# Two graph-attention networks on one core: the loops over edge batches written out on every engine, and the gather lists read from the SBUF table itself

## The chip, the cores and the metric

One NeuronCore of a Trainium2 chip runs the whole kernel. The metric is the device time of one execution in microseconds (us); lower is better.

## What is computed

The reference takes 3125 nodes with 256 features and 53125 edges, sorted by target node. It runs one graph network of two attention layers (4 heads, then 1 head), adds the input and normalises each row, then a second network of one attention layer with 8 heads and edge features, adds and normalises again. In each layer

```python
e = leaky_relu(alpha_s[src] + alpha_d[dst], 0.2)      # + edge term in the third layer
m = segment_max(e, dst)
w = exp(e - m[dst])
out = segment_sum(h[src] * (w / segment_sum(w, dst)[dst]), dst) + bias
```

where `h = x @ W`, per head. So there are three attention layers, which the kernel numbers 0, 1 and 2.

## The kernel before

**Tiling.** The 3125 nodes are 25 blocks of 128 rows, one node per partition. The edges are cut into 440 slots of 128 edges, so that all targets of a slot lie in one block. Eleven slots (B) form a batch, and a layer has 40 batches (K). For every slot GpSimd gathers the 128 source rows from a table in DRAM with one indirect DMA (L1128), TensorE sums the weighted rows into their targets by a product with a one-hot matrix (L1485), and VectorE adds the result to the block's sums in SBUF (L766). In layers 0 and 1 the scores need only a small transposed computation for each batch. In layer 2 every slot also has an edge encoding: four matmuls (L1496, L1499), a ReLU on ScalarE (L1280), a product and a reduction on VectorE (L772, L778).

**Order of the work.** Each engine has its own instruction stream, with the order of a batch's period written out by hand (the table `AT` says at which slot a step is put). VectorE's period begins with `rescale` (L747), reads the block numbers of the next batch's slots into registers once (`load`, L787), and uses them as offsets into `sums`. Four batches are in flight: a period works on batch t and on its successors t+1, t+2 and t+3. Buffers such as `rows` are rings of three (RING), and the batch's place in the ring is `u`.

**The loops.** On VectorE, ScalarE, TensorE and GpSimd `batches` runs the period. Batches 0 to 35 of a layer are 12 turns of a hardware loop, whose body holds three periods, one for each `u`. Batches 36 to 39 follow the loop, written out, with batch numbers known when the program is built. In the loop a semaphore's target value depends on the loop's register, so waits compare against registers, which instructions ahead of them compute (L295, L304), and the loop ends in a compare and a branch (L340). Batch 36 is the only written-out one that still does all of a full period's steps, since it still has three batches behind it. SyncE loads what a batch needs (`meta`), also in a loop over batches 3 to 38.

**The gather lists.** The row numbers of all 440 slots lie in SBUF in `index_all`. The gathers of batches 0 to 2 read them from there. From batch 3 on, SyncE first copies the batch's 11 columns to `index`, a ring of three, and GpSimd waits for that copy (`s_index`) and reads its list from the ring. A batch's gathers also wait until TensorE has used the rows of the batch three before it in the same buffer (`agg`).

Of the kernel before, what the change touches and what calls it, by code (L numbers as in the profile page):

```python
# [21 lines left out]
I32 = mybir.dt.int32  # L22
# [5 lines left out]
P = 128  # L28
# [8 lines left out]
B = 11  # L37
K = SLOTS // B
# [3 lines left out]
RING = 3  # L42
# [55 lines left out]
def gat_kernel(nc, x, src, dst, edge_attr, w1, as1, ad1, b1, w2, as2, ad2, b2, w3, as3, ad3, edge_w, edge_b, b3, out):  # L98
    ctx = ExitStack()
    with ctx:  # L100
        def sb(name, shape, dt=F32):
            return ctx.enter_context(nc.sbuf_tensor(name, shape, dt))
# [4 lines left out]
        def sem(name):  # L107
            return ctx.enter_context(nc.semaphore(name))
# [21 lines left out]
        flags = sb("flags", [8 * B, RING, 5, P])  # L130
        chain = sb("chain", [1, RING, 2, 8, B + 1])
        carry = sb("carry", [2, RING, P])
        index = sb("index", [P, RING, B], I32)
        index_all = sb("index_all", [P, SLOTS], I32)
        blk = sb("blk", [1, K * BPAD], I32)
        ntab = sb("ntab", [P, BLOCKS, 16])
# [144 lines left out]
        s_dpad = sem("s_dpad")  # L281
        s_w0 = sem("s_w0")
        s_parts = sem("s_parts")
        s_index = [[sem(f"s_index{l}_{u}") for u in range(RING)] for l in range(3)]
        s_meta = [[sem(f"s_meta{l}_{u}") for u in range(RING)] for l in range(3)]
        s_rows = [[sem(f"s_rows{l}_{u}") for u in range(RING)] for l in range(3)]
        s_tab = [[sem(f"s_tab{l}_{u}") for u in range(TROW)] for l in range(3)]
# [9 lines left out]
        def need_apart(eng, *waits):  # L297


            for w, c in waits:  # L300
                if isinstance(w, str):
                    need(eng, w, c)
                else:
                    eng.wait_ge(w, c)  # L304
                if not isinstance(c, int):
                    eng.sem_inc(s_passed[eng], 1)
# [29 lines left out]

        def batches(eng, body):

            loops = (K - 3) // RING
            with eng.Fori(0, loops) as j:  # L340
                for u in range(RING):
                    body(Batch(j, u), K)
            for k in range(loops * RING, K):
                body(Batch(k // RING, k % RING), K - k)

        def block_regs(eng, tag):
# [545 lines left out]
        def _(sp):  # L892
# [42 lines left out]
            for l in range(3):  # L935
                H = HEADS[l]

                def meta(t, l=l, H=H):
                    if not isinstance(t.j, int) or t.k >= RING:

                        need_apart(sp, ("fac", l * K + t.k - 2), ("hot", l * K + t.k - 2),
                                   ("mask" if SELF[l] else "diff", l * K + t.k - 2),
                                   (s_rows[l][t.u], t.j * (16 * B)))
                    if not isinstance(t.j, int) or t.k >= RING:
                        sp.dma_start(index[:, t.u, :], index_all[:, bass.ds(t.k * B, B)]).then_inc(s_index[l][t.u], 16)
                    for h in range(H):
                        sp.dma_start(flags[h * B:(h + 1) * B, t.u, :, :].rearrange("p t e -> p (t e)"),
                                     flags_d[bass.ds(t.k * B, B), :]).then_inc(s_meta[l][t.u], 16)
                    for i, at in ((0, 1), (1, 0)):
                        row = chain_d[i:i + 1, bass.ds(t.k * B, B)]  # L950
                        sp.dma_start(chain[0:1, t.u, i, 0:H, at:at + B],
                                     row.unsqueeze(1).to_broadcast([1, H, B])).then_inc(s_meta[l][t.u], 16)
                    sp.dma_start(carry[:, t.u, :], carry_d[bass.ds(t.k * B, 1), :, :].rearrange("a r e -> (a r) e")).then_inc(s_meta[l][t.u], 16)
                    sp.dma_start(locb[:, t.u, :], loc_d[bass.ds(t.k * B * P, B * P)].partition_broadcast(P)
                                 ).then_inc(s_meta[l][t.u], 16)
                    if l == 2:
                        for i in range(3):
                            sp.dma_start(attrT[9 * i:9 * i + 9, t.u, :],
                                         attrT_d[:, bass.ds(t.k * B * P, B * P)]).then_inc(s_meta[l][t.u], 16)
# [18 lines left out]
                else:  # L978
                    need(sp, "add", l * K * B)
                    first_metas()  # L980
                    for b in range(BLOCKS):
                        write(b, b % TROW)
                with sp.Fori(1, K // RING) as j:
                    for u in range(RING):
                        meta(Batch(j, u))
                for k in range(K // RING * RING, K):
                    meta(Batch(k // RING, k % RING))
                if l < 2:

# [16 lines left out]
        def _(pool):  # L1006
# [62 lines left out]
            for l in range(3):  # L1069
# [49 lines left out]

                def gather(t, l=l):  # L1120
                    old = not isinstance(t.j, int) or t.k >= RING
                    if old:
                        need_apart(pool, (s_index[l][t.u], t.j * 16))
                    for lo, hi in GATHERS:
                        if old:
                            need_apart(pool, ("agg", (t.k + (l * K - 3)) * B + hi))
                        for s in range(lo, hi):
                            g.indirect_dma_start(out=rows[:, t.u, s, 0:ROW[l]], out_offset=None, in_=table[l],  # L1128
                                                 in_offset=bass.IndirectOffsetOnAxis(ap=index[:, t.u, s:s + 1] if old else index_all[:, t.k * B + s:t.k * B + s + 1], axis=0)
                                                 ).then_inc(s_rows[l][t.u], 16)  # L1130
                for k in range(RING):
                    gather(Batch(0, k))
# [443 lines left out]
```

## Time and profile before

| what | us |
|---|---|
| median of 3 runs | 2442.32 (2439.75 to 2443.36) |
| the profiled execution, its own time | 2431.28 |
| its span, first to last instruction | 2429.4 |
| layer 0, from its first `rescale` to its last gather | 131 to 670 |
| layer 1, from its first gather to its last | 774 to 1333 |
| layer 2, from its first `rescale` to that of batch 36 | 1494 to 2332 |

The positions are in us from the start of the span. The rows further down come from this one execution; PE is TensorE, DVE VectorE, ACT ScalarE, POOL GpSimd and SP SyncE; DVEq is VectorE's instruction queue, where register operations show. "issue" as the releaser of an engine means that the engine waited for no other engine or transfer that the trace shows. Between the layers lie stages that are written out already and that the change leaves alone.

### The profile page before, as it was taken

The numbers are of one execution on the slowest core, as the hardware profiler recorded it, in microseconds if no ns is written. First come the engines' busy times: TensorE is split into PE (matmuls) and PEld (weight loads), VectorE is DVE, ScalarE is ACT, GpSimd is POOL, SyncE is SP. The second block draws the span as 40 slices with busy tenths as digits, with TensorE's granted clock in tenths as the row PEclk, the third lists the DMA queues.
The fourth block names the chain that finished last, engine by engine and source line by source line (L and its number), as shares of the span: only waits on it lengthen the run. The fifth ranks groups of instructions, "written<-read, shape, count | busy, mean of one in ns | idle before, by whom it ended". The sixth has DMA issues, their size and how long they took to land.

```text
span 2429.4 us, 49749 instructions
## 1 busy us (share of the span) xinstructions
PE 1753.2 (72%) x8878; PEld 1055.8 (43%) x8879; DVE 1844.4 (76%) x5643; ACT 1018.6 (42%) x3430; POOL 1535.4 (63%) x1675
## 2 busy tenths in 40 slices
PE   4368777778765677777787667778777777787783
PEld 3245444444433354444454433444444444444441
DVE  5478888888896566666666766888888888888888
ACT  2233444344424354454454443444444444444444
POOL 2567777777745777777777474565555555655553
PEclk9578888888868788888887776788787787888876
DMA  5644444444612444544446122333333333333321
GB/s 153 150 129 133 139 139 143 137 136 138 192 35 72 131 131 131 137 131 132 136 131 175 57 71 79 86 107 92 91 103 86 104 89 94 107 88 97 102 69 54
DMA packets 145430, 273.39 MB, mean 113 GB/s; under 512 B 55607, under 2 KB 80306, under 8 KB 145289
## 3 DMA queue, kind: packets, MB, share of 16 engines
q0 software_dynamic: 64704, 182.91, 27.6%
q1 hardware_dynamic: 77452, 86.16, 11.8%
q10 hardware_dynamic: 3158, 3.20, 0.4%
q14 instruction: 96, 0.79, 0.1%
q8 instruction: 20, 0.33, 0.1%
HBM read 255.35 MB, written 17.20 MB: 112 GB/s over the span
## 4 chain that ended last, share of the span: by engine, by line
PE 30%; DVE 27%; issue 19%; POOL 9%; DVEq 6%; ACT 4%; DMA 4%; SPq 2%; POOLq 0%; ACTq 0%
PE bank L1485 15%; POOL rows L1128 7%; DVE sums L766 5%; PE bank L1499 5%; PE bank L1419 3%; DVE prod L772 3%; DVE dots L778 3%; DVE rows L755 3%; DVEq L787 3%; PE bank L1496 2%; DMA rows<-table,index 2%; DVEq L766 1%; ACT rows L1273 1%; DVE adsum L639 1%; DVE onehotT L629 1%
## 5 line engine op out<-in xcount | busy, mean ns | idle before, releaser
L1128 POOL DMA_INDIRECT rows<-table,index x1221 | 1190.4, 975 | 636.6 <-PE bank L1485 321.6
L1485 PE MATMUL bank<-rows,onehot 128*128 128x264 f32 (+1 forms) x2640 | 1015.6, 492 | 198.2 <-DVE sums L766 143.6
L766 DVE TENSOR_TENSOR sums<-sums,bank 128x264 f32 (+1 forms) x1320 | 552.6, 419 | 190.8 <-PE bank L1485 139.2
L1485 PEld LDWEIGHTS bank<-rows,onehot 128*128 128x128 f32 x2640 | 510.1, 230 | 380.3 <-DVE sums L766 207.2
L1273 ACT ACTIVATE rows<-rows,wgt 128x33 f32<-128x33 f32 (+2 forms) x1520 | 443.9, 369 | 0.2
L1280 ACT ACTIVATE prod<-bank 128x256 f32<-128x256 f32 x440 | 168.3, 383 | 408.3 <-PE bank L1499 406.9
L1228 ACT CAST onehot<-bank 128x768 f32<-128x768 bf16 x240 | 178.0, 743 | 331.5 <-PE bank L1419 328.6
L1499 PE MATMUL bank<-late,onehotT 128*128 x1320 | 259.8, 314 | 0.0
L755 DVE TENSOR_TENSOR rows<-rows,wgt 128x260 f32<-128x260 f32 (+2 forms) x560 | 240.1, 429 | 3.6 <-ACT wgt L1266 3.6
L772 DVE TENSOR_TENSOR prod<-prod,bank 128x256 f32<-128x256 f32 x440 | 182.5, 415 | 46.6 <-ACT prod L1280 43.7
L1419 PE MATMUL bank<-identb,onehotT 128*128 128x128 bf16 x1320 | 160.0, 278 | 37.3 <-DVE onehotT L629 30.5
L778 DVE TENSOR_REDUCE dots<-prod 128x8 f32<-128x256 f32 x440 | 181.6, 413 | 2.4
L1496 PE MATMUL bank<-edgew,late 30*128 30x256 bf16 x440 | 136.9, 311 | 60.9 <-DVE onehotT L629 60.1
L1419 PEld LDWEIGHTS bank<-identb,onehotT 128*128 128x128 bf16 x1320 | 125.1, 128 | 76.9 <-issue 52.2
L1441 PE MATMUL bank<-ident,score 128*44 128x128 f32 (+2 forms) x200 | 46.6, 302 | 151.1 <-DVE score L656 150.5
L1499 PEld LDWEIGHTS bank<-late,onehotT 128*128 128x128 bf16 x1320 | 101.7, 104 | 78.8 <-issue 30.6
L1128 POOL DMA_INDIRECT rows<-table,index_all x99 | 98.2, 992 | 59.2 <-issue 29.1
L1235 ACT COPY scoreT<-bank 44x256 f32<-44x256 f32 (+2 forms) x120 | 39.6, 330 | 227.1 <-PE bank L1441 220.4
L1496 PEld LDWEIGHTS bank<-edgew,late 30*128 30x128 bf16 x440 | 44.1, 100 | 187.3 <-DVE onehotT L629 85.7
L1140 POOL TENSOR_TENSOR rows<-rows,wgt 128x264 f32<-128x264 f32 x160 | 102.6, 672 | 33.2 <-ACT wgt L1266 32.5
L1258 ACT ACTIVATE expT<-expT 44x256 f32<-44x256 f32 (+2 forms) x120 | 45.4, 378 | 171.3 <-DVE expT L727 171.1
L1402 PE MATMUL bank<-wts,rows 128*128 128x264 f32 (+2 forms) x300 | 97.1, 456 | 18.6 <-DVE wts L388 11.0
(196 smaller groups left out, 1937.7 us busy)
## 6 DMA issues: line engine op xcount, KB each, us to landing
locb<-loc_d SPq DMA_DIRECT2D x120, 352.0 KB
rows<-table,index POOLq DMA_INDIRECT x1221
flags<-flags_d SPq DMA_DIRECT2D x520, 27.5 KB
table<-rows SPq DMA_DIRECT2D x25, 136.0 KB, 1.7
table<-rows SPq DMA_DIRECT2D x25, 134.0 KB, 2.4
late<-table SPq DMA_DIRECT2D x1, 3300.0 KB, 18.0
table<-rows SPq DMA_DIRECT2D x25, 129.5 KB, 2.0
late<-table SPq DMA_DIRECT2D x1, 3212.5 KB, 18.3
```

The source lines that it names most:

```text
L755: done(v.tensor_tensor(r, r, w.to_broadcast([P, H, n]), ALU.mult), "mulv")
L766: done(v.tensor_tensor(a, a, ps_sum[l][s % len(ps_sum[l])][:, 0:VV], ALU.add), "add")
L772: done(v.tensor_tensor(prod[:, s % 3, :], prod[:, s % 3, :], ps_enc[s % 3][:, D:2 * D], ALU.mult), "prod")
L778: done(v.tensor_reduce(dots[:, t.u, s, :], prod[:, s % 3, :].rearrange("p (h c) -> p h c", h=8), AX.X, ALU.add), "dot")
L1128: g.indirect_dma_start(out=rows[:, t.u, s, 0:ROW[l]], out_offset=None, in_=table[l], in_offset=bass.IndirectOffsetOnAxis(ap=index[:, t.u, ...
L1228: done(a.copy(onehot[:, t.u, lo:hi, :].rearrange("p s e -> p (s e)"), ps_hotb[l][g][:, 0:(hi - lo) * P]), "hotT")
L1273: i = a.activation(r, r, ACT.Copy, scale=wgt[:, t.u, h * B + s:h * B + s + 1])
L1280: done(a.activation(prod[:, s % 3, :], ps_enc[s % 3][:, 0:D], ACT.Relu), "enc")
L1419: r = m.transpose(ps_hotb[l][g][:, (s - lo) * P:(s - lo + 1) * P], onehotT[:, t.u, s * P:(s + 1) * P], identb[:, :])
L1485: done(m.matmul(ps_sum[l][s % nb][:, 0:VV], onehot[:, t.u, s, :], rows[:, t.u, s, 0:VV], start=True, stop=True), "agg")
L1496: m.matmul(p[:, 0:D], attrT[:, t.u, s * P:(s + 1) * P], edgew3[:, :], start=True, stop=True)
L1499: r = m.matmul(p[:, D:2 * D], onehotT[:, t.u, s * P:(s + 1) * P], hnode3[:, bass.ds(b, 1), i, :].rearrange("p a f -> p (a f)"), start=(i = ...
```

## The change

`batches` no longer makes a loop: all 40 batches of a layer are written out on the four compute engines, and SyncE's loop over `meta` likewise. Every batch number is then a constant, and so is every wait's target. The copies to `index`, the ring and its semaphores go, and all gathers read `index_all`. The reading of block numbers into registers (L787) stays.

```diff
-        index = sb("index", [P, RING, B], I32)
...
-        s_index = [[sem(f"s_index{l}_{u}") for u in range(RING)] for l in range(3)]
...
         def batches(eng, body):
 
-            loops = (K - 3) // RING
-            with eng.Fori(0, loops) as j:
-                for u in range(RING):
-                    body(Batch(j, u), K)
-            for k in range(loops * RING, K):
+            for k in range(K):
                 body(Batch(k // RING, k % RING), K - k)
...
-                    if not isinstance(t.j, int) or t.k >= RING:
-                        sp.dma_start(index[:, t.u, :], index_all[:, bass.ds(t.k * B, B)]).then_inc(s_index[l][t.u], 16)
...
-                with sp.Fori(1, K // RING) as j:
-                    for u in range(RING):
-                        meta(Batch(j, u))
-                for k in range(K // RING * RING, K):
+                for k in range(RING, K):
                     meta(Batch(k // RING, k % RING))
...
                     old = not isinstance(t.j, int) or t.k >= RING
-                    if old:
-                        need_apart(pool, (s_index[l][t.u], t.j * 16))
                     for lo, hi in GATHERS:
                         if old:
                             need_apart(pool, ("agg", (t.k + (l * K - 3)) * B + hi))
                         for s in range(lo, hi):
-                                                 in_offset=bass.IndirectOffsetOnAxis(ap=index[:, t.u, s:s + 1] if old else index_all[:, t.k * B + s:t.k * B + s + 1], axis=0)
+                                                 in_offset=bass.IndirectOffsetOnAxis(ap=index_all[:, t.k * B + s:t.k * B + s + 1], axis=0)
```

## Rows read from the trace of the kernel before

**Rows 1.** The page, part 1: each engine's busy time.

```profile
PE 1753.2 (72%) x8878; PEld 1055.8 (43%) x8879; DVE 1844.4 (76%) x5643; ACT 1018.6 (42%) x3430; POOL 1535.4 (63%) x1675
```

**Rows 2.** Busy time by stage, all engines; the stretch's length follows its bounds.

```profile
core 0: us, PE busy (x) PEld busy (x) DVE busy (x) ACT busy (x) POOL busy (x), PEclk, DMA share, GB/s
131.00:670.00 539.00, 417.11 (x2085) 259.38 (x2085) 447.22 (x1454) 219.18 (x778) 400.14 (x407) 0.84 0.50 142
774.00:1333.00 559.00, 417.41 (x2150) 262.57 (x2151) 353.46 (x1224) 259.61 (x721) 424.82 (x440) 0.81 0.50 136
...
1494.00:2332.00 838.00, 647.17 (x3530) 366.04 (x3530) 690.48 (x2017) 359.49 (x1260) 473.03 (x535) 0.80 0.34 95
```

**Rows 3.** POOL's groups from 774 to 1333: count, busy, mean ns, idle before.

```profile
L1128 POOL DMA_INDIRECT rows<-table,index x407 | 393.3, 966 | 124.1 <-issue 114.0 <-PE bank L1485 10.1
L1128 POOL DMA_INDIRECT rows<-table,index_all x33 | 31.5, 955 | 25.4 <-DMA table<-rows 15.6 <-issue 9.5 <-PE bank L1485 0.3
```

**Rows 4.** POOL in order of time, layer 1: start, duration, in brackets idle before.

```profile
773.98 0.98 POOL L1128 DMA_INDIRECT rows<-table,index_all  x1 [15.65 <-DMA table<-rows]
...
814.30 0.95 POOL L1128 DMA_INDIRECT rows<-table,index_all  x1 [0.30 <-issue]
815.55 0.95 POOL L1128 DMA_INDIRECT rows<-table,index  x1 [0.30 <-issue]
...
1331.71 0.95 POOL L1128 DMA_INDIRECT rows<-table,index  x1 [0.30 <-issue]
```

**Rows 5.** POOL's waits, 146 to 670: total us, times, longest.

```profile
POOL rows L1128 <- PE bank L1485: 23.4, 43, 2.2
```

**Rows 6.** DVE's waits in layer 2, 1520 to 2330.

```profile
DVE sums L766 <- PE bank L1485: 40.1, 40, 1.3
DVE sums L747 <- issue: 33.7, 11, 3.3
```

**Rows 7.** The chain around one turn of layer 2's loop: start, us, what.

```profile
1773.62 0.07 DVEq L340
1773.68 2.91 issue
```

**Rows 8.** The instruction queues' packets in layer 2's loop, 1520 to 2330.

```profile
q14 instruction: 57, 0.47, 0.2%
q8 instruction: 3, 0.05, 0.0%
```

**Rows 9.** DVE in order of time: `rescale` of batches 0, 33, 36 and 37, layer 2.

```profile
1494.78 0.43 DVE L747 TENSOR_TENSOR sums<-sums,bank 128x264 f32 x1 [1.50 <-issue]
...
2264.86 0.43 DVE L747 TENSOR_TENSOR sums<-sums,bank 128x264 f32 x1 [3.02 <-issue]
...
2331.82 0.43 DVE L747 TENSOR_TENSOR sums<-sums,bank 128x264 f32 x1
...
2353.24 0.42 DVE L747 TENSOR_TENSOR sums<-sums,bank 128x264 f32 x1
```

**Rows 10.** DVE's waits in layer 0, 146 to 650.

```profile
DVE sums L766 <- PE bank L1485: 24.2, 32, 1.1
...
DVE sums L747 <- issue: 2.9, 6, 0.5
```

**Rows 11.** Busy time by batch in layer 2: batches 31, 33 and 36.

```profile
2218.34:2240.18 21.84, 16.70 (x98) 9.49 (x98) 19.74 (x57) 10.06 (x35) 13.21 (x16) 0.96 0.35 101
...
2264.86:2287.16 22.30, 17.67 (x98) 10.22 (x98) 19.09 (x57) 9.95 (x35) 10.47 (x13) 0.81 0.30 82
...
2331.82:2353.24 21.42, 17.15 (x99) 10.43 (x99) 18.94 (x56) 9.95 (x35) 14.00 (x16) 0.82 0.28 77
```

**Rows 12.** DMA issues by line: the copies of the gather lists.

```profile
index<-index_all SPq DMA_DIRECT2D x111, 5.5 KB
```

**Rows 13.** The instruction queue's packets from 1360 to 1500, which is written out.

```profile
q14 instruction: 7, 0.06, 0.2%
```

**Rows 14.** DVE's waits from 1360 to 1500.

```profile
DVE sums L747 <- issue: 1.5, 1, 1.5
```

## The prediction, made before the changed kernel ran

> **What bounds the kernel now.** I read the page's busy shares first, only to see that they don't decide: VectorE leads with 76%, TensorE has 72%, GpSimd 63% [rows 1]. Busy time by stage does. In layer 1 VectorE is busy for 353 of 559 us, but GpSimd issues all 440 gathers of the layer in that stretch [rows 2]. A gather takes 0.966 us and the idle time ahead of it is 0.30 us, 124.1 us over 407 [rows 3]. The few waits named after TensorE come to about the same 0.30 us each, so they are the pitch and no wait. From 773.98 to 1331.71 GpSimd never stops [rows 4]: 439 steps in 557.7 us, 1.27 us each. Layer 1 is bound by the issue of gathers.
>
> Layer 0 is nearly so. From 146 to 670 GpSimd waits 43 times for TensorE's sums, 23.4 us in all [rows 5]. 43 × 0.30 = 12.9 us of that is pitch; 10.5 us are real waiting for rows to be used.
>
> Layer 2 is another case: 838 us for 36 batches, GpSimd busy 473 us, VectorE 690 us [rows 2]. There VectorE's stream sets the pace. Its waits show the largest single thing that is no work: 33.7 us ahead of `rescale`, in 11 places of about 3.06 us, with nothing to wait for [rows 6]. The chain tells where they come from: VectorE's queue executes the loop's last instruction, L340, and then stands still for 2.91 us [rows 7]. It is the turn of the loop, and 12 turns have 11 jumps back. Instruction packets arrive all through this stretch, 57 on the queue q14 [rows 8]. I take the gap for the fetch of the loop's first instructions after each jump.
>
> **The change, part by part, layer 2.** Its three parts here:
>
> *The jumps.* 11 × 3.06 = 33.7 us go from VectorE's stream. Does something else end the wait later? At the loop's exit, where the branch isn't taken, `rescale` of batch 36 at 2331.82 has no idle time ahead of it, while that of batch 33 has 3.02 us [rows 9]. So nothing waits behind the gap. I take all 33.7 us.
>
> *The price of a jump, weighed against a rule.* The row shows 2.91 us for one turn of layer 2 [rows 7]. The Trainium skill, page "Advanced Engine Details and Errata", section "Control Flow Timing", puts a compare-and-branch at about 108 ns; by that alone the 11 jumps would cost 1.2 us, and the forecast would be 32 us later. Its page "Runtime: NRT & Kernel Launch", section "Instruction fetch mechanics", adds that a taken branch to a target outside the window of fetched pages stalls for a fetch, which fits the row. In layer 0 the whole wait "issue" ahead of `rescale` is 2.9 us in 6 places [rows 10]: there a turn costs next to nothing, and I expect no such gain from layers 0 and 1.
>
> *Constants for registers.* Waits against constants need fewer queue instructions, on all engines at once, and they can go with the instruction they guard. The trace has one sample: batch 36 is written out and does a full period. It takes 2353.24 − 2331.82 = 21.42 us [rows 9]. A batch in the loop, without gaps: batches 0 to 35 take 2331.82 − 1494.78 = 837.0 us; less 33.7 for the jumps and 3 for the slow start of batch 0 (an estimate) it is 800 us, 22.2 us each. Batches 33 to 35 agree: 2331.82 − 2264.86 = 66.96, 22.3 us each. Work is the same, VectorE busy 19.09 us in batch 33 and 18.94 in batch 36 [rows 11]. So 0.8 us × 36 = 28.8 us. One sample is weak. The bounds: 0.2 us (7 us in all), since batch 31 too ran in 21.84 us with a granted clock of 0.96 [rows 11], and 1.4 us (50 us), which is under half of the 3.2 us that VectorE isn't busy in a batch of 22.3. I take the sample.
>
> *What hides less then.* TensorE is busy 17.2 to 17.7 us in such a batch, at a granted clock of 0.81 or 0.82 (a mean over its two levels, 1.2 and 2.4 GHz), and ScalarE 9.95 [rows 11]. Both fit under 21.4 us. GpSimd's 14.0 us do too.
>
> **Layers 0 and 1.** The turn of GpSimd's loop and its register work are hidden by the gathers: the idle time ahead of a gather stays 0.30 us everywhere in layer 1 [rows 3, 4]. The list's address changes nothing: the gather at 814.30 reads `index_all`, the next one `index`, both take 0.95 us after 0.30 us [rows 4], and the means are 955 and 966 ns [rows 3]. Layer 1: 0, bounds ±3 us for the few gathers that are longer than 0.95 us (440 × 0.95 = 418 against 424.8 busy).
>
> In layer 0 a quicker period on VectorE and TensorE brings forward the sums that GpSimd waits for, at most the 10.5 us worked out above; VectorE itself loses 24.2 us to TensorE there, both of them little slower than the gathers [rows 10]. With 0.8 us less in a batch I expect most of it back, 8 us; bounds 0 and 10.5.
>
> **SyncE and the copies.** 111 copies of 5.5 KB are no longer issued [rows 12], and GpSimd's wait for them goes. It never showed: every wait of the gathers is the pitch or TensorE [rows 3, 5]. The cover is that a list is copied while the ring's earlier batches are gathered. The metas behind each copy on SyncE's queue start a little earlier, for nobody. 0 us.
>
> **The sum.** 33.7 + 28.8 + 8 + 0 + 0 = 70.5 us. The profiled execution took 2431.3 us, of which 2429.4 are span, so it would take 2361. It ran 11 us below the median of the runs. Against the median 2442.3 the forecast is 2442.3 − 70.5 = 2372 us.
>
> **Rivals.**
>
> *The straight stream can't be fetched fast enough (slower).* Now every instruction has to be brought in once, in all three layers, and each late packet would stand an engine still for the 2.9 us of [rows 7]. In layer 2's loop 60 packets came in about 35 batches [rows 8], 1.7 for a batch. Were each of 1.7 × 40 = 68 exposed, it would be 197 us, less 70.5: 2569 us. From 24 exposed ones on (70.5 / 2.9) the change loses. For it: many more instructions are fetched. Against it: between 1360 and 1500 all is written out, 7 packets came on q14 [rows 13], and the longest wait of VectorE without another engine or a transfer behind it is 1.5 us [rows 14]; and in the loop itself all but the jump's own packets came unnoticed, 60 packets to 11 gaps [rows 6, 8]. The same Runtime page says that crossing a block's boundary is mostly hidden; by that this rival falls. Chance 0.04.
>
> *Only the jumps pay.* Batch 36 was quick for being late: SyncE has nothing more to load then. The constants would bring some 0.1 us a batch, layer 0 nothing: 2442.3 − 37 = 2405 us. For it: one sample, a DMA share of 0.28 against 0.30 to 0.35 [rows 11]. Against: it has fewer queue instructions for the same work. Chance 0.14.
>
> *The gap isn't the jump.* By the branch price of the errata page, something at the batch boundary would stand there in any case, such as the four waits of `rescale`; then only 28.8 + 8 us come, 2405.5 us. Against it: two in three boundaries of the loop have no gap, and neither has its exit [rows 6, 9]. Chance 0.02.
>
> *TensorE takes the gap back.* It catches up during the 3 us, and without them the period stays bound by it: VectorE waits 40.1 us for its sums in this layer already [rows 6]. If they grow by the 33.7 us and the constants bring nothing, it is 2442 us, no change. Against: 17.7 us of TensorE work for 22.3 us. Chance 0.03.
>
> *More than forecast.* The constants help by 1.4 us a batch and layer 0 in full: 33.7 + 50 + 10.5 = 94 us, 2348 us. Chance 0.09.
>
> The forecast has the rest, 0.68, for 2355 to 2395.
>
> **The range.** Its low end is the sum of the high bounds with 3 us from layer 1: 33.7 + 50 + 10.5 + 3 = 97, 2345 us. Its high end is 33.7 + 7 + 0 − 3 = 38, 2404 us; I move it to 2408, so that the two cases at 2405 lie inside. It leaves out the first and the fourth rival and the outer part of "more", about 0.1 in all. A measurement of this kernel tells 0.2% (5 us) from nothing. Slower takes the first rival, 0.04; within 0.2% the fourth, 0.03; faster the rest, 0.93.
>
> **What the profile after will show.** In layer 2 no idle time of 3 us ahead of `rescale`; its `rescale` instructions 21.4 us apart; in layer 1 the gathers still 1.27 us apart, from first to last about 558 us; in layer 0 GpSimd's waits for TensorE shorter by 8 us; more packets on the instruction queues, without engines idle for them. The prediction is wrong if gaps of 3 us turn up at places without a wait, if batches of layer 2 stay at 22.2 us, or if layer 1 gets shorter.

## The result, and the profile after

The changed kernel takes 2353.27 us (median of 4 runs, 2352.5 to 2355.57), the kernel before 2441.03 us on the same chip (4 runs, 2437.94 to 2443.36). The ratio is 0.9643 with a 95% interval of 0.9626 to 0.9659: 87.8 us less. The forecast was 70.5 us less, 2372 us, with a range of 2345 to 2408.

The profiled execution has a span of 2351.5 us, 77.9 less than that of before. So some 10 us of the 87.8 show in no trace: the profiled execution of before took 2431.28 us, 9.8 under the 2441.03 here (11 under the median that the prediction had), and the one of after took 2353.31 us, which is its median.

The page of the changed kernel, span and part 1, against [rows 1]:

```profile
span 2351.5 us, 42182 instructions
PE 1702.8 (72%) x8878; PEld 1045.5 (44%) x8878; DVE 1847.3 (79%) x5642; ACT 1018.0 (43%) x3430; POOL 1539.9 (65%) x1675
```

VectorE's work did not get less: it is busy for 1847.3 us, before for 1844.4; only its idle time went. TensorE does the same 8878 matmuls in 1702.8 busy us where it took 1753.2; its granted clock, a mean over the two levels of 1.2 and 2.4 GHz, is 0.807 over the execution against 0.796, and 0.85 in layer 2 against 0.80. That comes back below. The busy time by stage, which answers to [rows 2]; the stretches here follow each other and cover layer 0, layer 1, the step between, layer 2 and the tail:

```profile
core 0: us, PE busy (x) PEld busy (x) DVE busy (x) ACT busy (x) POOL busy (x), PEclk, DMA share, GB/s
135.00:664.00 529.00, 413.20 (x2097) 257.96 (x2096) 445.76 (x1452) 219.84 (x781) 400.77 (x408) 0.83 0.51 146
664.00:1319.00 655.00, 468.01 (x2362) 301.15 (x2362) 442.68 (x1429) 295.98 (x878) 464.91 (x491) 0.79 0.43 124
...
1480.00:2255.00 775.00, 613.27 (x3530) 358.84 (x3529) 693.71 (x2017) 358.45 (x1260) 484.55 (x535) 0.85 0.36 104
2255.00:2351.50 96.50, 49.89 (x203) 28.05 (x203) 81.28 (x261) 40.60 (x127) 39.32 (x53) 0.68 0.17 53
```

Measured from the same instruction to the same instruction in both traces (lines of after are 6 to 13 lower):

```
stretch                                              before    after   difference
layer 0, gather at 135.74 to the last (669.58)        533.8    524.2      -9.7
layer 1, first gather to last                         557.7    555.1      -2.7
layer 2, rescale of batch 0 to rescale of batch 36    837.0    774.3     -62.7
```

What ended VectorE's waits in and around layer 2, 1440 to 2270, against [rows 6] (total us, times, longest):

```profile
DVE sums L760 <- PE bank L1472: 31.8, 38, 1.1
DVE prod L766 <- ACT prod L1267: 18.9, 69, 1.2
DVE ends L683 <- PE bank L1435: 12.7, 37, 0.5
...
DVE sums L741 <- issue: 1.5, 2, 1.2
```

The 33.7 us ahead of `rescale` (now L741) are gone (1.2 of the 1.5 us left is the wait ahead of batch 0), and the wait for TensorE's sums is 31.8 us where it was 40.1. GpSimd's waits in layer 0, 146 to 660, against [rows 5]:

```profile
POOL rows L1115 <- issue: 111.2, 365, 0.3
POOL rows L1115 <- PE bank L1472: 14.6, 34, 1.4
```

34 × 0.30 us of the second row are the pitch between gathers, so 4.4 us are waiting; before it was 10.5. Layer 1 is still a row of gathers. GpSimd's group there, 760 to 1322, against [rows 3] (count, busy, mean ns, idle before):

```profile
L1115 POOL DMA_INDIRECT rows<-table,index_all x440 | 422.2, 960 | 149.7 <-issue 123.4 <-DMA table<-rows 16.0 <-PE bank L1472 10.4
```

The instruction queues' packets in layer 2, 1430 to 2260, against [rows 8]:

```profile
q8 instruction: 39, 0.64, 0.3%
q14 instruction: 54, 0.44, 0.2%
```

93 packets where 60 were, and no engine shows an idle time near 3 us for one: from batch 1 of layer 2 on the longest that ends with no other engine or transfer is 0.6 us on VectorE, 0.7 on ScalarE and 0.5 ahead of a matmul. So far every row does what the prediction said. One place does not. VectorE and then GpSimd at the head of batch 22 of layer 2, in order of time:

```profile
1950.97 0.42 DVE L741 TENSOR_TENSOR sums<-sums,bank 128x264 f32 x1
1951.49 0.59 DVE L623 TENSOR_SCALAR onehotT<-locb,pidx 128x1408 bf16<-128x1408 bf16 x1
1951.99 2.99 DVE L671 TENSOR_TENSOR_SCAN top<-flags,top 88x128 f32<-88x128 f32 x1
1954.91 0.40 DVE L760 TENSOR_TENSOR sums<-sums,bank 128x264 f32 x1
```

```profile
1951.33 0.94 POOL L1115 DMA_INDIRECT rows<-table,index_all  x1 [0.30 <-issue]
1952.28 2.41 POOL L1127 TENSOR_TENSOR rows<-rows,wgt 128x264 f32<-128x264 f32 x4
```

The backward scan of the edges' tops (L671, L677 before), 0.41 us where nothing is beside it, took 2.99 us and ended 0.3 us after GpSimd's four multiplications did (1954.98 and 1954.69). It is the only one of the 36 that took so long. In 33 batches it took 0.85 us, as in this one:

```profile
1738.75 0.85 DVE L671 TENSOR_TENSOR_SCAN top<-flags,top 88x128 f32<-88x128 f32 x1
```

```profile
1739.23 2.83 POOL L1127 TENSOR_TENSOR rows<-rows,wgt 128x264 f32<-128x264 f32 x4
```

That collision turned out to decide the experiments on the jumps.

### The profile page after: what moved, and what is told of

Its sections match the earlier page's. It is cut to its first block, busy times and chain, and to the rows that moved or that the text cites. A ratio compares the mean times of both kernels' runs of the same rounds, so it can differ in the third digit from the quotient of the medians.

```text
span 2351.5 us, 42182 instructions
## 1 busy us (share of the span) xinstructions
PE 1702.8 (72%) x8878; PEld 1045.5 (44%) x8878; DVE 1847.3 (79%) x5642; ACT 1018.0 (43%) x3430; POOL 1539.9 (65%) x1675
## 4 chain that ended last, share of the span: by engine, by line
DVE 31%; PE 28%; issue 16%; POOL 13%; DVEq 4%; DMA 3%; SPq 2%; ACT 2%; ACTq 0%; POOLq 0%
PE bank L1472 15%; POOL rows L1115 12%; DVE sums L760 8%; PE bank L1486 4%; DVE prod L766 4%; DVE rows L749 3%; PE bank L1406 3%; DVE dots L772 3%; DMA rows<-table,index_all 2%; PE bank L1483 2%; DVEq L781 2%; DVEq L760 1%; DVE onehotT L623 1%; PE bank L1419 1%; DVE adsum L633 1%
## 5 line engine op out<-in xcount | busy, mean ns | idle before, releaser
L1115 POOL DMA_INDIRECT rows<-table,index_all x1320 | 1283.2, 972 | 615.0 <-issue 346.5
L1472 PE MATMUL bank<-rows,onehot 128*128 128x264 f32 (+1 forms) x2640 | 989.6, 483 | 211.9 <-DVE sums L760 174.3
L1472 PEld LDWEIGHTS bank<-rows,onehot 128*128 128x128 f32 x2640 | 510.3, 229 | 371.0 <-issue 246.4
L1486 PE MATMUL bank<-late,onehotT 128*128 x1320 | 253.2, 308 | 0.0
L749 DVE TENSOR_TENSOR rows<-rows,wgt 128x260 f32<-128x260 f32 (+2 forms) x560 | 241.2, 431 | 3.5 <-ACT wgt L1253 3.5
L766 DVE TENSOR_TENSOR prod<-prod,bank 128x256 f32<-128x256 f32 x440 | 182.1, 414 | 27.8 <-ACT prod L1267 27.4
L772 DVE TENSOR_REDUCE dots<-prod 128x8 f32<-128x256 f32 x440 | 181.5, 413 | 2.4
L1428 PE MATMUL bank<-ident,score 128*44 128x128 f32 (+2 forms) x200 | 51.6, 330 | 124.9 <-DVE score L650 124.9
L1127 POOL TENSOR_TENSOR rows<-rows,wgt 128x264 f32<-128x264 f32 x160 | 112.8, 729 | 32.3 <-ACT wgt L1253 31.6
L1428 PEld LDWEIGHTS bank<-ident,score 128*44 128x44 f32 (+2 forms) x200 | 17.1, 110 | 174.6 <-DVE score L650 171.7
```

The source lines that it names most:

```text
L749: done(v.tensor_tensor(r, r, w.to_broadcast([P, H, n]), ALU.mult), "mulv")
L766: done(v.tensor_tensor(prod[:, s % 3, :], prod[:, s % 3, :], ps_enc[s % 3][:, D:2 * D], ALU.mult), "prod")
L772: done(v.tensor_reduce(dots[:, t.u, s, :], prod[:, s % 3, :].rearrange("p (h c) -> p h c", h=8), AX.X, ALU.add), "dot")
L1472: done(m.matmul(ps_sum[l][s % nb][:, 0:VV], onehot[:, t.u, s, :], rows[:, t.u, s, 0:VV], start=True, stop=True), "agg")
L1486: r = m.matmul(p[:, D:2 * D], onehotT[:, t.u, s * P:(s + 1) * P], hnode3[:, bass.ds(b, 1), i, :].rearrange("p a f -> p (a f)"), start=(i = ...
```

## The experiments

Each ratio is against the kernel before on the same chip in the same set of runs. Three chips' sets had the kernel before at 2439 to 2441 us. Two others had it at 2837 and 2838 us, with every kernel some 16% longer at a granted clock of 0.69 to 0.72 against 0.78 to 0.81; what makes these chips slower stays open. Layer spans are compared only within one kind. On the slower chips there is no profile of the kernel before, so the kernel with the hint, whose time is some 0.2% from it, stands in for it there.

### The jumps: a hint, and a longer body

**e1_hint, e1b_hint, e7_hint_again.** The kernel before, and VectorE's three loops get a hint that has the loop's head fetched before the jump. It adds one instruction to each loop, and nothing else:

```
-            with eng.Fori(0, loops) as j:
+            with nc.Fori(0, loops, 1, engines=[eng.engine],
+                         hint_back_edge=eng is nc.vector or eng.engine == nc.vector.engine) as j:
```

> The kernel before with one instruction added at the head of each of VectorE's three loops: a hint that its branch back will be taken, so that the target's instructions are fetched ahead. Loops, register waits and gather lists stay. If the 2.9 us after each jump of layer 2 are the fetch of the loop's head (my theory), the 11 gaps ahead of rescale go and the kernel is 30 to 35 us faster than before, 0.986 of its time; VectorE's waits named issue ahead of rescale in layer 2 fall from 33.7 us to under 3. If the gap is something else that stands at the batch boundary, the gaps stay and the time is that of before. If TensorE takes the gap back, the gaps go and the time is still that of before. Layers 0 and 1 don't move.

> The kernel with the fetch hint on VectorE's loops again, in the hope of a chip that grants TensorE the clock that the first two profiles had (0.80); on the chip of the first run it was 0.69, the kernel before took 2838 us, and the gaps went without any gain. At a clock of 0.80 my theory expects 25 to 35 us less than before (0.986 to 0.990), since there VectorE's stream sets layer 2's pace. If TensorE takes the gap back at any clock, the time is that of before.

> The fetch hint on VectorE's loops once more, for a chip that grants the clock of the first measurement (before at about 2441 us). There my theory expects 25 to 35 us less than before, 0.986 to 0.990. Where the kernel before takes 2837 us again, the time of before, as in the two runs already made.

Ratios: 1.0013 (0.9997 to 1.0029) and 1.0021 (1.0002 to 1.004) on the chips at 2838 and 2837 us, and 1.0093 (1.0059 to 1.0128) on a chip at 2441, where it is 2462.88 us. The first was expected to be 30 to 35 us faster and was not; the last, expected 25 to 35 us faster, is 22 us slower. The gaps went all the same. VectorE's waits in layer 2 of e7_hint_again, 1510 to 2290:

```profile
DVE prod L772 <- ACT prod L1280: 44.4, 88, 1.2
DVE sums L766 <- PE bank L1485: 36.6, 39, 1.3
DVE sums L747 <- issue: 5.5, 11, 0.5
```

11 waits of 0.5 us where 11 of 3.06 stood, so 28.2 of the 33.7 us are gone, and with them the packets: 2 on q14 from 1530 to 2350, where [rows 8] has 57. Yet layer 2 is 856.2 us long against 837.0. The gap is fetch time, and to take it away made the kernel slower.

**e2_body6.** The kernel before, six batches to a turn in place of three on the four compute engines: the 11 jumps of each layer fall to 5.

```
-            with eng.Fori(0, loops) as j:
-                for u in range(RING):
-                    body(Batch(j, u), K)
+            with eng.Fori(0, loops // 2) as j:
+                for u in range(2 * RING):
+                    body(Batch(j * 2, u), K)
```

> The kernel before with six batches to a turn of the loop in place of three, on the four compute engines: 6 turns and 5 jumps in a layer, still with register waits. If the gap is a fetch that comes with a loop body too long to stay in the engine's instruction memory, layer 2 has 5 gaps of 2.9 us in place of 11 (18 us less), and now VectorE also stands still for about 2.9 us after each of 5 jumps in layers 0 and 1, where a turn was free. Layer 1 is bound by the gathers and hides it, layer 0 hides most: 10 to 20 us faster than before, 0.992 to 0.996. If the gap has nothing to do with the body's length, layers 0 and 1 show no gap, and layer 2 has 5.

Ratio 1.0007 (0.9987 to 1.0027), where 0.992 to 0.996 was expected. Layer 2 was 886.6 us against 909.1 with the hint, but now VectorE stands still at each of the 5 jumps in all three layers. From the branch to the next instruction of VectorE's queue it is 2.84 to 3.56 us in layer 0, 3.40 to 3.89 in layer 1, 3.50 to 4.21 in layer 2. In the kernel before, the same distance is 0.22 to 0.30 us in layers 0 and 1, and 2.73 to 3.02 in layer 2. ScalarE's queue does likewise in layer 2: 2.47 to 2.85 us, where it is 0.18 in the kernel before. VectorE's waits in layer 1, 1000 to 1600, of e2_body6, and the packets of the same stretch:

```profile
DVE sums L747 <- issue: 20.8, 16, 4.2
```

```profile
q14 instruction: 35, 0.29, 0.2%
```

The same packets with the hint and the short body, in the same stretch:

```profile
q14 instruction: 1, 0.01, 0.0%
```

The layer does not matter, the length of the body does. Counted in the traces, a turn of VectorE's loop before has 278 instructions in layer 0, 257 in layer 1 and 369 in layer 2, its queue's own among them; with six batches it has 552, 510 and 734. The two shortest jump in 0.3 us, all others in 2.7 us or more. ScalarE's turn in layer 2 has 195 before and 387 with six batches. So a short body stays and a long one is fetched anew in every turn; between 278 and 369 no run has a body.

### Which engines, and the copies

**e4_vector_only, f4_vector_only_again.** VectorE's three loops alone are written out. **e5_all_but_vector.** Those of TensorE, ScalarE and GpSimd alone (with `!=`).

```
+            if eng.engine == nc.vector.engine:
+                for k in range(K):
+                    body(Batch(k // RING, k % RING), K - k)
+                return
             loops = (K - 3) // RING
```

> The kernel before with VectorE alone written out; TensorE, ScalarE, GpSimd and SyncE keep their loops and register waits. If VectorE's own stream set the pace of layer 2, nearly all of the gain comes: 33.7 us for the jumps, most of 28.8 us for the constants and some of layer 0, 55 to 75 us faster than before, 0.970 to 0.977. If the constants pay through the other engines (TensorE's register operations above all), only the jumps' 34 us come, 0.986.

> The reverse of VectorE alone: TensorE, ScalarE, GpSimd and SyncE... of these the first three are written out, VectorE (and SyncE) keep the loop, its jumps and register waits. At a clock of 0.80 the gaps ahead of rescale stay and VectorE keeps setting the pace of layer 2: 0 to 12 us faster than before. If the constants pay on TensorE, it is 20 us faster or more; on a chip with the clock at 0.69, where TensorE sets the pace, I expect that: 30 us or more.

> VectorE's three loops alone are written out, all other engines keep theirs; run before on a chip where every kernel took 16% longer. It differs from the kernel with the branch hint in VectorE's constants alone (waits and batch numbers known in the program), and from the changed kernel in the other engines' constants. If the constants on VectorE carry the gain, layer 2 stands near 775 to 800 us; if those of the other engines carry it, near 856 us, as with the hint; half and half, about 815 us. Layer 0 should be at the kernel before's 534 us if its gain is GpSimd's, TensorE's and ScalarE's.

**e3_ring_kept.** All loops written out, but the lists are still copied by SyncE to the ring `index`, and GpSimd waits for them.

> Everything written out as in the changed kernel, but the gather lists are still copied to the ring of three and GpSimd waits for the copies: the change without its second part. By my theory the copies were hidden and cost nothing: the time of the changed kernel, 0.964 of before, within 0.2%. If the copies or their wait mattered, it is slower than the changed kernel, up to the 20 us that layers 0 and 1 and the rest gained beyond layer 2.

**e6_changed_again.** The changed kernel once more.

> The changed kernel itself, beside the others. In the runs so far the kernel before took 2837 us, with a granted clock near 0.69, where the first measurement had 2441 us and 0.80. If the chip is again such a one, I expect the ratio of the written-out kernel with the ring kept, 0.967, within 0.003, since the copies of the lists cost nothing; at the clock of the first measurement 0.964.

```
kernel                 ratio (95% interval)        chip's before   layer 0   layer 1   layer 2
e3_ring_kept           0.9672 (0.9626 to 0.9717)   2838            634.7     711.5     840.5
e4_vector_only         0.9840 (0.9817 to 0.9863)   2838            662.9     701.7     862.1
e1_hint                1.0013 (0.9997 to 1.0029)   2838            666.3     702.7     909.1
e5_all_but_vector      0.9891 (0.9857 to 0.9925)   2837            640.2     692.7     902.3
e1b_hint               1.0021 (1.0002 to 1.0040)   2837            670.9     702.6     906.9
e6_changed_again       0.9665 (0.9629 to 0.9701)   2441            523.6     556.2     776.1
f4_vector_only_again   0.9758 (0.9738 to 0.9777)   2439            532.0     556.2     793.8
the kernel before      1                           2441            533.8     557.7     837.0
```

Expected were 0.970 to 0.977 for VectorE alone, which came on the faster chip (0.9758) and not on the slower one (0.9840); 30 us or more on a slow chip for the other three, which came (31 us by the ratio); and the change's own ratio for the last two, which came within their intervals. Layer 0's gain is not VectorE's: with VectorE alone written out it is 532.0 us, with all of them 523.6; on the slower chips the other three engines alone bring it from about 668, with the hint, to 640. Layer 2's is VectorE's first: 43 of 63 us. The kernel that keeps ring and copies gains as much as the change, within the intervals (on another chip, and with an interval of 13 us to either side, so that less than that can't be told). Its layer 1 is the longest of its kind at 711.5 us, but behind its first gather every wait there ends on the semaphore of TensorE's sums, and none on that of a copy.

### The collision

In all kernels so far GpSimd's four weight multiplications of layer 2 stand at the head of a batch, behind the last gathers of the batch before. Three kernels, the one before, the one with the hint and the changed one, each with one edit: the next batch's multiplications are issued ahead of the last group of three gathers, in the middle of VectorE's batch.

```
                 def gather(t, l=l, first=None):
                     ...
                     for lo, hi in GATHERS:
+                        if first is not None and lo == GATHERS[-1][0]:
+                            muls(first)
...
-                    for s in OWN[l]["P"]:
-                        mul(t, s)
-                    if left > 3:
-                        gather(t.after(3))
+                    if left > 3:
+                        gather(t.after(3), first=t.after(1))
+                    elif left > 1:
+                        muls(t.after(1))
+                muls(Batch(0, 0))
```

> The kernel before, loops kept, with one edit: GpSimd's four weight multiplications of the next batch in layer 2 stand ahead of the last group of three gathers of a batch, in place of at the head of the next batch. There VectorE's backward scan of the last edges can run beside them: it took 538 ns on average in the kernel before, 1279 ns with the branch hint, against 410 ns when it runs alone. Theory A (the scan loses its time to GpSimd's multiplications): the scan falls to about 0.42 us and layer 2 gains up to 36 x 0.12 = 4 us where nothing else waits; the three gaps per turn of the loop stay. Theory B (the mean of the scan has another cause, its input arrives late): the scan stays at 538 ns and the time does not change. The last three gathers of a batch leave some 2.4 us later; if that is what the scores wait for, the kernel gets up to 36 x 2.4 = 86 us slower.

> The kernel with the branch hint on VectorE's loops and the same move of GpSimd's multiplications. With the hint alone layer 2 was 856.2 us against 837 and the scan took 44.8 us in place of 18.8. Theory A (the collision eats the gap's time): the scan falls to 0.42 us, 30 us come back, and layer 2 ends at about 826 us or under, some 10 us or more below the kernel before, as the 33.7 us of gaps are now gained in part. Theory B (what the gap hid is TensorE's and ScalarE's lateness, and the long scan only stands where VectorE would have waited anyway): the scan gets short and layer 2 stays within 5 us of 856, with the waits for the banks and for ScalarE's products grown by as much.

> The changed kernel with the same move of GpSimd's multiplications. Its scan took 897 ns on average, 31.4 us in 35 batches. Theory A: the scan falls to about 0.42 us, layer 2 gains up to 17 us and the kernel is at about 2340 us, the fastest of all. Theory B: the scan gets short, the wait for the banks that TensorE fills grows by as much, and the time stays at 2355 us within 5 us.

Medians 2443.78, 2430.8 and 2374.63 us; ratios 1.0021 (1.0005 to 1.0037), 0.9967 (0.9952 to 0.9983), 0.9724 (0.9702 to 0.9746). Only the second did what one of its theories said: its layer 2 is 819.7 us, under the 826 of theory A. The first was to gain up to 4 us and lost 5; the third was to end at 2340 or 2355 us. VectorE's scan L677 in layer 2, 1510 to 2290, in the kernel before, with the hint, and with hint and move (count, busy, mean ns, idle before):

```profile
L677 DVE TENSOR_TENSOR_SCAN top<-flags,top 88x128 f32<-88x128 f32 x34 | 18.4, 540 | 0.0
```

```profile
L677 DVE TENSOR_TENSOR_SCAN top<-flags,top 88x128 f32<-88x128 f32 x32 | 40.7, 1273 | 0.0
```

```profile
L677 DVE TENSOR_TENSOR_SCAN top<-flags,top 88x128 f32<-88x128 f32 x34 | 13.9, 408 | 0.0
```

And how it comes about, first VectorE and then GpSimd, at one turn of the loop with the hint:

```profile
1716.66 0.43 DVE L747 TENSOR_TENSOR sums<-sums,bank 128x264 f32 x1 [0.50 <-issue]
1717.13 0.59 DVE L629 TENSOR_SCALAR onehotT<-locb,pidx 128x1408 bf16<-128x1408 bf16 x1
1717.63 3.07 DVE L677 TENSOR_TENSOR_SCAN top<-flags,top 88x128 f32<-88x128 f32 x1
```

```profile
1717.05 0.95 POOL L1128 DMA_INDIRECT rows<-table,index  x1 [0.30 <-issue]
1718.02 2.41 POOL L1140 TENSOR_TENSOR rows<-rows,wgt 128x264 f32<-128x264 f32 x4
```

The same place in the kernel before:

```profile
1704.09 0.42 DVE L778 TENSOR_REDUCE dots<-prod 128x8 f32<-128x256 f32 x1
1707.60 0.43 DVE L747 TENSOR_TENSOR sums<-sums,bank 128x264 f32 x1 [3.09 <-issue]
1708.06 0.59 DVE L629 TENSOR_SCALAR onehotT<-locb,pidx 128x1408 bf16<-128x1408 bf16 x1
1708.57 0.85 DVE L677 TENSOR_TENSOR_SCAN top<-flags,top 88x128 f32<-88x128 f32 x1
```

```profile
1706.36 2.79 POOL L1140 TENSOR_TENSOR rows<-rows,wgt 128x264 f32<-128x264 f32 x4
```

In the kernel before GpSimd had begun its multiplications in the gap and was 2.2 us into 2.8 us of them when the scan began (1708.57 − 1706.36). The scan met only their end, here and in 8 more batches behind a jump. Without the gap it meets them all. Both times it ends 0.27 us after they do (1720.70 and 1720.43, 1709.42 and 1709.15).

How much it costs hangs on a tenth of a microsecond. With the hint 11 scans began 0.36 to 0.39 us ahead of GpSimd's first multiplication and took 3.06 to 3.08 us. In the changed kernel 31 began 0.47 to 0.50 us ahead and took 0.85 (1738.75 and 1739.23 above); there GpSimd's first multiplication got longer instead, 0.86 us where it has some 0.65. The one that began 0.29 us ahead is that of batch 22, with its 2.99 us.

The two tables below are means over batches 0 to 35 of layer 2, worked out from the starts of VectorE's instructions, in us. The first gives a batch's length by its place in the turn of three, with the scan's own mean in brackets (written-out kernels have no turn):

```
                        1st              2nd              3rd (ends with the jump)
the kernel before       22.60 (0.74)     22.33 (0.40)     24.82 (0.46)
hint                    26.16 (2.85)     22.44 (0.42)     22.75 (0.50)
before, moved           22.66 (0.41)     22.43 (0.41)     25.08 (0.41)
hint, moved             22.91 (0.41)     22.51 (0.40)     22.88 (0.41)
```

The hint takes 2.07 us from the batch that ends with the jump and gives 3.56 to the one that follows. With the multiplications out of the way it takes 2.20 and gives 0.25.

The second cuts a batch into five pieces of VectorE's stream: from `rescale` over the scan to the first product (L772) behind it; on to the product behind the batch's fourth weight multiplication (L755), with waits for ScalarE's products in it; from there to the sum (L766) that waits for TensorE's bank; the rest; and the last step, from the batch's last reduction (L778) to the next `rescale`, with the jump in it:

```
                        head    to middle   wait    rest    last step   batch
the kernel before       2.81    11.07       1.59    6.43    1.34        23.25
hint                    3.35    11.63       1.57    6.68    0.56        23.78
before, moved           2.84    10.98       1.57    6.64    1.36        23.39
hint, moved             2.84    11.07       1.55    6.75    0.56        22.77
VectorE alone           2.79    11.14       1.47    6.30    0.35        22.05
changed                 2.77    10.84       1.27    6.28    0.35        21.51
changed, moved          2.71    10.84       1.32    6.73    0.34        21.94
```

The hint wins 0.78 in the last step, loses 0.54 in the head, where the scan is, 0.56 behind it and 0.25 in the rest. Behind the head TensorE, which works in order, had stood for the scan's result, which it never did in the kernel before; that is 0.29 us a batch. TensorE's wait in layer 2 with the hint, 1510 to 2290:

```profile
PE bank L1448 <- DVE top L677: 10.6, 10, 1.1
```

With the move, the first two losses are gone (2.84 and 11.07); the last stays (6.75), as the move costs something there itself (6.64 against 6.43 without the hint). Of the 19 us by which the hint lengthened layer 2, the first batch of a turn has 12 × 3.56 = 42.7, from which the saved gaps go. The granted clock in layer 2 was 0.77 with the hint, against 0.80 before and 0.80 with hint and move; what it added by itself stays open.

In the changed kernel the move gains nothing. The head falls by 0.06 only, though its scan falls from 883 to 413 ns, since what comes next there waits for ScalarE's product anyway: 0.16 us behind a scan of 0.85, 0.73 behind one of 0.41. And in the rest of the batch, where GpSimd's multiplications now are, 0.45 is lost. VectorE's fifth weight multiplication and its forward scan (L663) meet them there and take 755 and 520 ns on average, where they took 423 and 414. At one place, VectorE and then GpSimd:

```profile
1703.32 0.74 DVE L749 TENSOR_TENSOR rows<-rows,wgt 128x264 f32<-128x264 f32 x1
1703.98 0.41 DVE L766 TENSOR_TENSOR prod<-prod,bank 128x256 f32<-128x256 f32 x1
1704.31 0.52 DVE L663 TENSOR_TENSOR_SCAN top<-flags,scoreT 88x128 f32<-88x128 f32 x1
```

```profile
1702.51 2.74 POOL L1129 TENSOR_TENSOR rows<-rows,wgt 128x264 f32<-128x264 f32 x4
```

So theory A holds for the hint. For the change neither does: the scan's time was hidden, as B says, but the move brought new collisions that neither theory had. f3_after_moved is 16 us slower than e6_changed_again (on another chip; the ratios are 0.9724 and 0.9665), and the changed kernel stays the fastest of all.

## Why the prediction was right

**The jumps: 33.7 us, and it was 35.6.** The last step of a batch fell from 1.34 to 0.35 us, 36 × 0.99 = 35.6 us in layer 2, in the changed kernel and in the one with VectorE alone alike, and in neither did another piece grow by more than 0.07. The 11 gaps are 33.7 of it; the rest lies in last steps that had no gap. That the gap is the fetch after a jump is shown from both sides: by the hint (gap and packets go) and by the longer body (gap and packets come, in layers that had none). A jump took 0.22 to 0.30 us where the body was short, and 2.7 to 4.2 where it was long. The Trainium skill, page "Runtime: NRT & Kernel Launch", section "Instruction fetch mechanics", has the stall after a jump out of the fetched window, and these runs agree. The Trainium skill's page "Advanced Engine Details and Errata", section "Control Flow Timing", has about 108 ns for a compare-and-branch; by that alone the 11 jumps would have given 1.2 us, and they gave 33.7.

But the argument "nothing waits behind the gap" was too quick. It rested on the loop's exit, where the gap was missing and nothing came in its place. 28.2 of the same 33.7 us, taken away by the hint alone, left the kernel 22 us slower. What stood behind it was no wait, and so the views of waits of the kernel before could not show it: an instruction of VectorE that gets longer when it runs beside one of GpSimd's. The prediction had no rival for it; its only case on the slower side, at 0.04, was another mechanism. That the change did not fall into it is luck as far as the prediction goes, for its reasoning would have taken the hint's 28 us for a gain just as well. In the changed kernel most scans start 0.1 us earlier against GpSimd than behind the hint's jumps. They take 0.85 us, which a wait for ScalarE's product covers, and only one takes 2.99; in that batch the head is 4.60 us long where most have 2.64. Had they all been so, it would have been some 70 us (35 × 1.96, an estimate from these two numbers), most of the gain.

**The constants: 28.8 us, and it was 27.** What is left of the batch fell by (23.25 − 1.34) − (21.51 − 0.35) = 0.75 us, × 36 = 27 us. The one sample, batch 36, was a good one: its 21.42 us against a mean of 21.51 after. The experiments split it. VectorE written out brings (23.25 − 1.34) − (22.05 − 0.35) = 0.21 us a batch, 7.6 us; the rest of the change 22.05 − 21.51 = 0.54, 19.4 us, of which 0.20 in the wait for TensorE's bank and 0.30 on the way to it. The prediction had not said whose constants, and expected at e4_vector_only most of the 28.8 us from VectorE's.

That these 19.4 us are all the constants' is not shown, for the granted clock in layer 2 rose with them: 0.80 before, 0.82 with VectorE alone, 0.85 with the change. Within the changed kernel, of batches 1 to 35 without batch 22, the 11 with the highest granted clock (0.91 on average) take 20.84 us and the 11 with the lowest (0.82) 21.79. That is about 0.1 us for each 0.01, so 0.03 would be 0.3 of the 0.54 us (an estimate from these rows). Whether shorter waits raised the clock, which would make that part the constants' after all, no run tells.

**Layer 0: 8 us, and it was 9.7.** GpSimd's waiting fell by 10.5 − 4.4 = 6.1 us; the rest lies in the gathers' own length, 396.2 us in sum where they took 399.7, which the prediction did not have. Its reason was half right: sums come earlier, but not from VectorE's side (532.0 us with VectorE alone against 524).

**Layer 1: 0 ± 3, and it was 2.7.** 439 steps of 1.264 us in place of 1.270: gathers of 960 ns in place of 966 and 955. It is inside the bounds, though the prediction's last sentence took a shorter layer 1 for a sign of being wrong.

**The copies: 0.** e3_ring_kept has them all and its ratio is 0.9672 (0.9626 to 0.9717) against 0.9643 and 0.9665. They cost nothing that these runs can tell, which is to within some 13 us.

**The sum.** 62.5 us in layer 2 were forecast, 62.7 came, 1.9 more from the last steps and 1.8 less from the rest; with 8 and 0 against 9.7 and 2.7, and 2.8 us at the edges of the layers, the profiles differ by 77.9. The time's further 10 us are the distance between a profiled execution and its median. It had been seen (11 us below) and carried over whole, to 2372 from the 2361 that the sum gave for the profiled execution; after the change the distance is nothing. Of the 19 us by which the forecast was high, that is 11. Why the profiled execution of before was so quick is open.

**The rivals.** *The stream can't be fetched* is refuted: 93 packets and no gap. *Only the jumps pay* is refuted: outside the last step a batch fell by 0.75 us and not by 0.1. With the hint it was the jumps that did not pay. *The gap isn't the jump* is refuted by e2_body6 and the hints. *TensorE takes the gap back*: with the multiplications moved, the hint should gain 0.80 us a batch in the last step and gains 0.62 in the whole (22.77 against 23.39); 0.18 is taken back, a quarter. The 13 us between 2443.78 and 2430.8 are what the jumps alone are worth then, in the profiles' layer 2 it is 22.4 us, but the profiled execution with the hint ran 8 us below its median. With the hint alone more than all was taken back, most of it through the long scan.

## What to carry to other kernels

To remove an idle gap is not yet to win it: look also at what another engine does meanwhile, and which instruction of yours will then run beside it; a view of waits does not show it, a row whose mean duration grows does. A loop body that was too long to stay fetched cost 2.7 to 4.2 us a turn here, and a hint or straight code removed it; whether that pays is read from the batch that follows. Cutting a batch into pieces by the starts of one engine's instructions, over all batches, splits a gain between its pieces better than sums of waits; the granted clock belongs beside every such piece.

## What the runs showed of the hardware that was not expected

- VectorE's scan over 88x128 elements (L677) takes 0.41 us alone. Beside GpSimd's multiplications of 128x264 it takes 0.85 us when it began 0.44 to 0.50 us ahead of them, and 2.96 to 3.09 when it began 0.27 to 0.40 us ahead, over all traces here; then it ends 0.3 us after the last of the four.
- VectorE's own multiplication L755 (L749 after), of the same size as GpSimd's, takes 0.42 us alone, 0.55 to 0.58 on average where the two overlap in kernels without the move, and up to 0.99 in those with it. The copies of 1x8 into `ends` (L692) go from 0.15 to as much as 1.6 us. The products and the reductions (L772, L778) take the same 0.41 to 0.42 us beside GpSimd as alone.
- In layer 2 VectorE's idle time ahead of `rescale` at a jump is 0.50 us with the hint and 2.98 to 3.27 without. From the branch to the next instruction of its queue it is 0.17 to 0.19 us with the hint, 2.73 to 3.02 without, and 0.22 to 0.30 without it in layers 0 and 1, with their shorter bodies.
- TensorE's aggregation of 128x264 (L1485, L1472 after) takes 474 to 486 ns on average in layer 2 when TensorE runs its loop, at a granted clock of 0.77 to 0.82, and 443 when it is written out, at 0.84 to 0.85. Whether the clock follows from the shorter waits or the other way round stays open.
- The same kernel takes 2441 us on some chips and 2838 on others.
